# Third norm of a graph-network kernel: three blocks in flight, two chunks summed within it, and three DMA queues in a new order

## The chip, the cores and the metric

The kernel runs on one core of one Trainium2 chip. The metric is the device time of one execution in microseconds; each version is run several times and the median is compared.

## What the reference computes

The input is a matrix x of 3125 nodes by 128 features and a list of 100,000 edges (src, dst). Four graph networks follow one another, each behind a row-wise layer norm and a ReLU, and each adds to x:

```
h = max(layernorm(x), 0);  x = x + L0(h)     # sum over edges, two-layer network, log-softmax
h = max(layernorm(x), 0);  x = x + L1(h)     # two normalised graph convolutions
h = max(layernorm(x), 0);  x = x + L2(h)     # 4 layers: (A h + h) W1, ReLU, W2, batch norm, ReLU
h = max(layernorm(x), 0);  x = x + L3(h)     # h W0, S h W1, S S h W2; batch norm; the same again; a projection
```

A is the adjacency matrix of the edges. S is the transposed one with self loops, scaled on both sides by the inverse root of the degrees. What the change touches lies between the last layer of L2 and the first sum of L3: the last batch norm and ReLU of L2, the addition to x, the layer norm with its ReLU (this is the third norm after the first one), and the first product with S.

## The kernel before, in words

The adjacency matrix lies in SBUF as 25 tiles (`ADJ`, 125 rows by 3125 columns in bf16). A sum over edges is a dense product on TensorE: for a chunk of up to 4 tiles of target nodes (500 columns) it runs through the 25 tiles `t` of source nodes, with two matmuls for each: one with the high part and one with the low part of the node features, both 16 bit, which lie in `HP`. There are `NC` = 7 chunks, so a full sum has 350 matmuls (`sum_tiles`, line 1159). In L2 the chunks have 4, 4, 4, 4, 4, 3 and 2 tiles (`SPANS`), in the first sum of L3 the order is reversed: 2, 3, 4, 4, 4, 4 and 4 tiles (`SPANS3`), that is 250, 375 and five times 500 columns.

L3 needs the transposed adjacency `ADJT`. It is written over `ADJ` by seven DMA transposes from a copy in DRAM (`turned(c)`, line 1668), one for each chunk of columns. A transpose of chunk c may start when the last layer of L2 has summed its chunk c, since it overwrites those columns. The copy in DRAM is made earlier (`keep`, counted by `s_kept`).

L2's batch norm works feature by feature on the transposed data in `Zf`. After its factors are known (`s_bn["ab"]`), the work goes on in `NB` = 5 blocks of `BT` = 5 tiles: `relu(b)` on ScalarE (line 1878), `turn_block` on TensorE (five fp32 transposes into PSUM, line 1958, into one of the two slots of `RB3`), and on VectorE the addition to x (line 1986). Then comes the third norm of that block in `third_norm` on VectorE and `third_high` on ScalarE: statistics (lines 1100 and 1993), a square root on ScalarE (line 2014), a reciprocal and three small products on VectorE (lines 1999 to 2005). ScalarE then writes the high part of the five tiles to `HP` (line 2018) and, in fp32, four of the five tiles again to a scratch tile `GZ` (line 2024). VectorE makes the fifth (line 1973) and subtracts: low part = fp32 value minus high part (line 1979). There is one scratch tile, so ScalarE writes it only when the low part of the block before is done.

The L3 sum of TensorE waits block by block for `E3["hp"]`. Between the matmuls of chunk c, at set tiles `t`, TensorE does the dense products of chunk c-1, the hooks: `hidden1` (t = 4, line 2189), `back1` (t = 6, line 2195), `turned_h` (t = 12, line 2204) and `hidden0` (t = 17, line 2210). Each hook waits for results that VectorE and ScalarE make of the one before. `hidden1` waits for `E3["red"]` of its chunk, an operation of VectorE (line 2133) that multiplies the sum by a row of degree factors.

Queues are written out by hand. That of SyncE, in the stretch of interest, holds in this order: the last `row_piece` (line 1662), the transposes 0 to 3, `rows_out(s1_d)` (line 1658, a column of factors written to DRAM as 3125 numbers of 4 bytes), the transposes 4 and 5, the weights of L3 (line 2090, `s_wt`), transpose 6, and the six degree rows (`row_in`, line 2076), each a row of up to 500 numbers read for all 128 partitions. VectorE's first line 2133 waits for all six. The queue of ScalarE brings the first row of `s1_d` when the whole third norm is done.

Of the kernel before, what the change touches and what calls it, by code (L numbers as in the profile page):

```python
# [53 lines left out]
def build(nc, a, out):  # L54
# [75 lines left out]
    with ctx:  # L130
# [202 lines left out]
        s_dt, s_home, s_row = sem("s_dt"), sem("s_home"), sem("s_row")  # L333
# [727 lines left out]
        def layers(role, e, general, line):  # L1061
            pe, act, dve, pool, sp = (role == r for r in ("pe", "act", "dve", "pool", "sp"))
            done = lambda s, n: e.wait_ge(s, n + 1)
            if pool:
# [63 lines left out]
            def first_of(v, c, spans=SPANS):  # L1128
                return v[:, 0:spans[c][1] * PN]

# [17 lines left out]
            def sum_tiles(E_, H, c, accs, turned, group, before, spans=SPANS):  # L1148

                j0, nt = spans[c]  # L1150
                for t in range(NT):
                    before(t)
                    if turned:
                        cols = ADJT[0:PN, t, j0 * PN:(j0 + nt) * PN]
                    else:
                        cols = ADJ[0:PN, t, j0 * PN:(j0 + nt) * PN]
                    for q in range(2):
                        two = accs[0] is not accs[1]
                        mm = e.matmul(accs[q], H[0:PN, t, q, 0:P], cols, start=(t == 0 and (two or q == 0)),  # L1159
                                      stop=(t == NT - 1 and (two or q == 1)), skip_group_check=general)  # L1160
                if general:
                    for j in range(j0, j0 + nt):
                        with e.Fori(0, NT) as t:
                            remainder_landed(group, j * NT + t + 1)
                            for q in range(2):
                                mm = e.matmul(accs[q][:, (j - j0) * PN:(j - j0 + 1) * PN],
                                              H[0:PN, bass.ds(t, 1), q, 0:P].rearrange("p o f -> p (o f)"),
                                              LOT[0:PN, 0:PN], start=False, stop=True, skip_group_check=True)
                            mm.then_inc(s_lom, 1)
                    e.wait_ge(s_lom, (group * NT + j0 + nt) * NT + 1)  # L1170
                    e.sem_inc(E_["agg"], 1)
                else:
                    mm.then_inc(E_["agg"], 1)

# [476 lines left out]
            if sp:  # L1651
# [163 lines left out]
            def layer2(l, last):  # L1815
# [42 lines left out]
                if act:  # L1858
# [92 lines left out]
            def turn_block(l, b, ring=RB):  # L1951

                e.wait_ge(s_bn["rel"], l * NB + b + 1)
                if b >= 2:
                    done(E2["hp"], l * NB + b - 1)
                for m in range(BT):
                    c = (b * BT + m) * PN
                    mm = e.transpose(ring[b % 2][0:PN, m * P:(m + 1) * P], Zf[:, c:c + PN], IDF[:, :])  # L1958
# [5 lines left out]
            RB3 = [PS[:, 0:2, :].rearrange("p b c -> p (b c)"), PS[:, 2:4, :].rearrange("p b c -> p (b c)")]  # L1964
            MINE3 = BT - 1

            def third_norm():

                def low(b):
                    zb = GZ[0:PN].rearrange("p (t f) -> p t f", f=P)  # L1970
                    for m in range(MINE3, BT):
# [3 lines left out]
                    line.sync()  # L1975
                    done(E3["hi"], (b + 1) * BT)
                    e.wait_ge(s_z3, (b + 1) * MINE3)
                    ts = slice(b * BT, (b + 1) * BT)
                    e.scalar_tensor_tensor(out=HP[0:PN, ts, 1, 0:P], in0=zb, scalar=0.0, in1=HP[0:PN, ts, 0, 0:P],
                                           op0=ALU.max, op1=ALU.subtract).then_inc(E3["hp"], 1)  # L1980

                for b in range(NB):
                    ts = slice(b * BT, (b + 1) * BT)
                    e.wait_ge(s_bn["tr"], (LAYERS - 1) * NB + b + 1)
                    xb = XR[0:PN, ts, :]
                    line(e.tensor_tensor(xb, xb, RB3[b % 2][0:PN, 0:BT * P].rearrange("p (t f) -> p t f", f=P), ALU.add))
# [9 lines left out]
                    if b:  # L1996
                        low(b - 1)
# [10 lines left out]
                low(NB - 1)  # L2008

            def third_high(b):  # L2010

                ts = slice(b * BT, (b + 1) * BT)
                e.wait_ge(s_stat3, b + 1)
                e.activation(SDV[0:PN, ts], MV[0:PN, ts, 1], ACT.Sqrt, bias=EPSC[0:PN]).then_inc(s_sd3, 1)
                e.wait_ge(s_rs3, b + 1)
# [4 lines left out]
                if b:  # L2020
                    done(E3["hp"], b)
                for m in range(MINE3):
                    j = b * BT + m
# [9 lines left out]
            if pe:  # L2033
                for b in range(NB):
                    turn_block(LAYERS - 1, b, RB3)
            bank4 = PS[:, 4, :].bitcast(BF16)
# [37 lines left out]
            def row_in(tile, v, c, spans, to=s_dib):  # L2074
                j0, nt = spans[c]
                e.dma_start(first_of(tile, c, spans), bcast(v[j0 * PN:(j0 + nt) * PN])).then_inc(to, 16)

            def beside(c):

                return Zf[:, SPANS3[c + 1][0] * P:] if c + 1 < NC else GAT  # L2080

            def y1_of(c):
                return beside(c) if c + 1 < NC else LOS

            if sp:
                e.wait_ge(s_dout, 118)
                done(E2["agg"], NC * LAYERS)
                turned(NC - 2)
                done(E2["d2"], NC * LAYERS)
                e.dma_start(WB[:, 0:2 * P].rearrange("p (q n) -> p q n", q=2),  # L2090
                            a["L3_gnn_l1_w"][0:2].rearrange("q p n -> p q n")).then_inc(s_wt, 16)

                turned(NC - 1)
                e.wait_ge(s_bn["tr"], LAYERS * NB)
                for c in range(NC - 1):
                    row_in(beside(c), di_d, c, SPANS3)
# [26 lines left out]
            if dve:  # L2123
                for k in range(NC):
# [3 lines left out]
                    if k == 0:  # L2128
                        e.wait_ge(s_dib, dib0 + 16 * (NC - 1))
# [54 lines left out]
            if pe:  # L2184
# [29 lines left out]
                e.wait_ge(s_wt, wt0 + 16)  # L2214
                for c in range(NC):
                    def before(t):
                        if c == 0 and t % BT == 0:
                            done(E3["hp"], t // BT + 1)
                        if c == 1 and t == 0:
                            done(E2["hp"], LAYERS * NB)  # L2220
# [77 lines left out]
            if dve:  # L2298
                def joined(c):
# [3 lines left out]
                    e.wait_ge(s_dib, dib0 + 16 * (NC - 1) + 16 * n)  # L2303
# [296 lines left out]
```

## Time and profile before

| what | value |
|---|---|
| median of 3 runs | 1275.43 us (1274.34 to 1275.48) |
| the profiled execution, its own time | 1283.77 us |
| its span | 1282.1 us |
| TensorE busy | 1138.4 us, 89% of the span |
| VectorE, ScalarE, GpSimd busy | 686.7, 455.7, 8.5 us |
| mean granted clock of TensorE | 0.966 of full speed |

The profiled execution is 0.65% longer than the median. PE is TensorE's matmuls and PEld its weight loads, DVE is VectorE, ACT is ScalarE, POOL is GpSimd and SP is SyncE; an engine's name with a q is its queue, where DMAs are issued. A granted clock of 0.50 is 1.2 GHz and 1.00 is 2.4 GHz.

### The profile page before, as it was taken

The numbers are of one execution on the slowest core, as the hardware profiler recorded it, in microseconds if no ns is written. First come the engines' busy times: TensorE is split into PE (matmuls) and PEld (weight loads), VectorE is DVE, ScalarE is ACT, GpSimd is POOL, SyncE is SP. The second block draws the span as 40 slices with busy tenths as digits, with TensorE's granted clock in tenths as the row PEclk, the third lists the DMA queues.
The fourth block names the chain that finished last, engine by engine and source line by source line (L and its number), as shares of the span: only waits on it lengthen the run. The fifth ranks groups of instructions, "written<-read, shape, count | busy, mean of one in ns | idle before, by whom it ended". The sixth has DMA issues, their size and how long they took to land.

```text
span 1282.1 us, 19431 instructions
## 1 busy us (share of the span) xinstructions
PE 1138.4 (89%) x6308; PEld 660.5 (52%) x6308; DVE 686.7 (54%) x2175; ACT 455.7 (36%) x1348; POOL 8.5 (1%) x31
## 2 busy tenths in 40 slices
PE   1677899998979999998998998992699997899997
PEld 1556677664644555545445445451455554444644
DVE  8999999995452235545363453556144334532211
ACT  1558988895561112212113113116121113631100
POOL 1000000000000000000000000000000000000000
PEclk9999999999999999998998998995799998999999
DMA  3100000001001023333232231699622213410001
GB/s 62 32 2 2 2 2 10 2 1 46 6 11 24 21 54 74 88 70 74 42 68 55 51 85 30 139 198 213 153 60 63 85 38 80 111 47 23 13 24 29
DMA packets 208801, 70.31 MB, mean 55 GB/s; under 512 B 180999, under 2 KB 208074, under 8 KB 208699
## 3 DMA queue, kind: packets, MB, share of 16 engines
q1 hardware_dynamic: 121131, 43.37, 14.8%
q10 hardware_dynamic: 87568, 25.67, 9.4%
q8 instruction: 52, 0.85, 0.3%
q14 instruction: 50, 0.41, 0.1%
HBM read 20.71 MB, written 28.26 MB: 38 GB/s over the span
## 4 chain that ended last, share of the span: by engine, by line
PE 75%; DVE 10%; DMA 4%; SPq 4%; ACT 3%; issue 3%; DVEq 1%; ACTq 0%; POOL 0%; POOLq 0%
PE PS L1159 50%; PE PS L889 7%; DVE HPb L753 3%; SPq L1668 3%; PE PS L2425 2%; PE PS L1456 2%; PE PS L878 2%; PE PS L854 2%; PE PS L1922 2%; PE PS L1928 2%; DMA deg_d<-ADJ 1%; DVE HPb L704 1%; ACT HPb L2402 1%; DMA di_d<-SM 1%; ACT ADJ L925 1%
## 5 line engine op out<-in xcount | busy, mean ns | idle before, releaser
L1159 PE MATMUL PS<-ADJ,HPb 125*128 125x500 bf16 (+2 forms) x2450 | 490.5, 356 | 8.8 <-DMA WB<-in_L_gnn_l_w 4.3
L1159 PEld LDWEIGHTS PS<-ADJ,HPb 125*128 125x128 f16 x2450 | 240.4, 98 | 254.3 <-issue 40.5
L925 ACT CAST ADJ<-PS 126x72 f32 (+7 forms) x784 | 193.1, 315 | 51.6 <-PE PS L889 18.4
L1159 PE MATMUL PS<-ADJ,Zf 125*128 125x500 bf16 (+2 forms) x1050 | 202.1, 352 | 0.0
L889 PE MATMUL PS<-HPb 128*128 128x150 bf16 (+3 forms) x784 | 191.0, 345 | 3.6 <-ACT ADJ L925 2.5
L1159 PEld LDWEIGHTS PS<-ADJ,Zf 125*128 125x128 f16 x1050 | 102.4, 97 | 93.8 <-issue 1.3
L753 DVE TENSOR_SCALAR HPb<-XRf,Zf 128x176 bf16<-128x176 f16 (+2 forms) x588 | 135.2, 289 | 1.0 <-PE PS L889 0.2
L878 PEld LDWEIGHTS PS<-HPb 128*128 128x128 bf16 x642 | 86.0, 141 | 59.7 <-issue 34.3
L1727 DVE CUSTOM_DVE_ANT_0 HPb<-ADJ,HPb 125x625 bf16<-125x625 bf16 x125 | 101.2, 810 | 3.7
L878 PE MATMUL PS<-HPb 128*128 128x25 bf16 x642 | 90.9, 214 | 13.2 <-DVE HPb L753 12.5
L1826 DVE TENSOR_SCALAR Zf<-PS,B_L 128x500 f32<-128x500 f32 (+2 forms) x28 | 19.1, 682 | 141.5 <-PE PS L1928 141.5
L889 PEld LDWEIGHTS PS<-HPb 128*128 128x128 bf16 x784 | 86.0, 160 | 6.2 <-ACT ADJ L925 5.7
L1863 ACT ACTIVATE STW<-PS,SM 128x500 f32<-128x500 f32 (+2 forms) x28 | 17.7, 632 | 194.5 <-PE PS L1159 194.5
L704 DVE TENSOR_TENSOR HPb<-XRf,Zf 128x1750 bf16<-128x1750 f16 x56 | 59.6, 1064 | 0.6 <-DVEq L801 0.3
L753 DVE TENSOR_SCALAR HPb<-HPb,Zf 128x526 bf16<-128x526 f16 x196 | 54.4, 353 | 0.0
L2425 PE MATMUL PS<-HPb 128*125 128x384 f32 x114 | 42.4, 518 | 11.3 <-ACT HPb L2402 11.3
L1958 PE MATMUL PS<-IDF,Zf 128*125 128x128 f32 x100 | 20.7, 364 | 30.6 <-ACT Zf L1878 30.6
L883 PE MATMUL PS<-HPb 128*128 128x25 bf16 x142 | 26.6, 230 | 14.2 <-DVE HPb L753 13.2
L2171 ACT ACTIVATE HPb<-XRf,SM 125x128 f32<-125x128 f32 x25 | 10.4, 484 | 77.3 <-PE PS L2195 77.3
L2425 PEld LDWEIGHTS PS<-HPb 128*125 128x125 f32 x114 | 20.8, 195 | 32.3 <-ACT HPb L2402 20.8
L1868 ACT ACTIVATE SFG<-PS,B_L 128x500 f32<-128x500 f32 (+2 forms) x28 | 17.7, 632 | 54.2 <-PE PS L1922 54.2
L1958 PEld LDWEIGHTS PS<-IDF,Zf 128*125 128x125 f32 x100 | 18.5, 264 | 34.3 <-ACT Zf L1878 33.1
(325 smaller groups left out, 1022.9 us busy)
## 6 DMA issues: line engine op xcount, KB each, us to landing
adj_d<-ADJ ACTq DMA_DIRECT2D x25, 700.0 KB
HPb<-y_d SPq DMA_DIRECT2D x19, 187.5 KB, 2.5
HPb<-di_d SPq DMA_DIRECT2D x10, 250.0 KB, 3.8
adj_d<-ADJ ACTq DMA_DIRECT2D x25, 81.2 KB
ADJ<-in_x SPq DMA_DIRECT2D x1, 1562.5 KB
q_d<-HPb SPq DMA_DIRECT2D x25, 62.5 KB
HPb<-di_d SPq DMA_DIRECT2D x5, 305.2 KB
HPb<-s_d ACTq DMA_DIRECT2D x5, 250.0 KB, 3.9
```

The costliest lines, as they stand in the source:

```text
L704: e.tensor_tensor(OHP[h][:, 0:PN, :], IOC[:, 0:PN, :], PTH[:, n0:n0 + HC].rearrange("p (o c) -> p o c", o=1) .broadcast_to([P, PN, HC]), A ...
L753: e.tensor_scalar(OHK[k][:, 0:KWS[q]], IOK[q], KT[:, n0 + m:n0 + m + 1], None, ALU.is_equal)\
L854: mm = e.matmul(ACC0[c], PIECES[t][0:PN, q, :], ADJ[0:PN, t, j0 * PN:(j0 + nt) * PN], start=(r == 0), stop=(r == 2 * NT - 1), skip_group_c ...
L878: mm = e.matmul(to[:, :, bass.ds(places[g], 1)].rearrange("p t o -> p (t o)"), lhs, OHK[m % RING][:, 0:NT], start=False, stop=True, skip_g ...
L883: e.matmul(CPS[h][:, g * NT:(g + 1) * NT], lhs, OHK[m % RING][:, 0:NT], start=(c == 0), stop=(c == GC - 1), skip_group_check=True)
L889: e.matmul(WPS[group % BANKS][:, 0:rests * NT], OHP[h][:, :, g * GC + c], OHK[m % RING][:, NTP:KWS[q]], start=(c == 0), stop=(c == GC - 1) ...
L925: e.copy(to, WPS[group % BANKS][0:PD, t0 * RESTS[q]:t1 * RESTS[q]] .rearrange("p (t d) -> p t d", t=t1 - t0)).then_inc(s_mv, 1)
L1159: mm = e.matmul(accs[q], H[0:PN, t, q, 0:P], cols, start=(t == 0 and (two or q == 0)), stop=(t == NT - 1 and (two or q == 1)), skip_group_ ...
L1668: e.dma_start(ADJT[:, :, s0:s1], adj_d[s0:s1].rearrange("s t d -> s (t d)"), transpose=True)\
L1727: line(e.tensor_tensor_reduce(out=JUNK[0:PN], in0=ADJ[0:PN, t, r * PIECE:(r + 1) * PIECE], in1=ROWP[0:PN], scale=1.0, scalar=0.0, op0=ALU. ...
L1958: mm = e.transpose(ring[b % 2][0:PN, m * P:(m + 1) * P], Zf[:, c:c + PN], IDF[:, :])
L2425: mm = e.matmul(PS[0:PN, 4 + k % 2, 0:3 * P], YT[k][:, q, 0:PN], VW[:, q * 3 * P:(q + 1) * 3 * P], start=(q == 0), stop=(q == 2))
```

## The change

Third norm:
- TensorE's transposes go through three PSUM slots in place of two. It issues blocks 0 to 2 at once, and 3 and 4 from within the L3 sum.
- ScalarE does all five `relu` first. For each block it then makes the five tiles once, in fp32, into one of two scratch tiles (`ZB3`), and copies the whole block to the 16-bit high part in one operation. It also makes the next block's square root.
- VectorE makes no tile of its own. The order of its work is statistics of block b, low part of block b-2 (now a subtraction of two tensors), factors of block b.

L3 sum: chunks 0 and 1 are summed together (`sum_pair`), tile by tile, while the norm delivers blocks. The hooks of chunk 0 move from chunk 1 to chunk 2, those of chunks 1 and 2 into chunks 3 and 4, those of chunk 3 into chunk 4; from chunk 5 on they are where they were.

Queues: transpose 0 goes ahead of the last `row_piece`, `rows_out(s1_d)` behind transpose 4; the weights of L3 move from SyncE's queue to ScalarE's, and TensorE waits for them ahead of chunk 2 in place of chunk 0; the six degree rows move to GpSimd's queue, where they wait for the fifth transposed block and not for the transposes of the matrix. The row of chunk 0 goes to a place of its own in `LOS`.

The diff, cut to its core:

```diff
+            def beside(c):
+                return LOS[:, 2 * P:] if c == 0 else later_part(c) if c + 1 < NC else GAT
+            def y1_of(c):
+                return later_part(c) if c + 1 < NC else LOS
+            def later_part(c):
+                return Zf[:, SPANS3[c + 1][0] * P:]
+            def degree_rows():
+                e.wait_ge(s_dout, 118)
+                e.wait_ge(s_bn["tr"], LAYERS * NB)
+                for c in range(NC - 1):
+                    row_in(beside(c), di_d, c, SPANS3, s_drow)
...
                 else:
                     home()
+                    degree_rows()
...
+            def sum_pair(E_, H, group, before):
+                for t in range(NT):
+                    before(t)
+                    for c in range(2):
+                        j0, nt = SPANS3[c]
+                        for q in range(2):
+                            mm = e.matmul(sums3(c), H[0:PN, t, q, 0:P], ADJT[0:PN, t, j0 * PN:(j0 + nt) * PN],
+                                          start=(t + q == 0), stop=(t + q == NT), skip_group_check=True)
+                        if t == NT - 1 and not general:
+                            mm.then_inc(E_["agg"], 1)
...
                 for r in range(1, NB):
+                    if r == NB - 1:
+                        e.wait_ge(s_kept, 16 * (2 * NT + 1))
+                        done(E2["agg"], (LAYERS - 1) * NC + 1)
+                        turned(0)
                     e.wait_ge(s_dout, 17 * (r + 1))
                     row_piece(di_d, r)
...
-                e.wait_ge(s_kept, 16 * (2 * NT + 1))
-                for c in range(NC - 2):
-                    if c == NC - 3:
-                        e.wait_ge(s_dout, 102)
-                        rows_out(s1_d, DEG)
+                for c in range(1, NC - 2):
                     done(E2["agg"], (LAYERS - 1) * NC + c + 1)
                     turned(c)
+                e.wait_ge(s_dout, 102)
+                rows_out(s1_d, DEG)
...
                         if b + 1 < NB:
                             relu(b + 1)
-                        if last:
-                            third_high(b)
-                        else:
+                        if not last:
                             e.wait_ge(s_bn["tr"], l * NB + b + 1)
                             high_part("L2", b, turned_block(b))
+                    if last:
+                        done(E2["d2"], NC * LAYERS)
+                        e.dma_start(WB[:, 0:2 * P].rearrange("p (q n) -> p q n", q=2),
+                                    a["L3_gnn_l1_w"][0:2].rearrange("q p n -> p q n")).then_inc(s_wt, 16)
+                        for b in range(NB):
+                            third_high(b)
...
-                if b >= 2:
-                    done(E2["hp"], l * NB + b - 1)
+                if b >= len(ring):
+                    done(E2["hp"], l * NB + b + 1 - len(ring))
...
-            RB3 = [PS[:, 0:2, :].rearrange("p b c -> p (b c)"), PS[:, 2:4, :].rearrange("p b c -> p (b c)")]
-            MINE3 = BT - 1
+            RB3 = [PS[:, 2 * k:2 * k + 2, :].rearrange("p b c -> p (b c)") for k in (0, 1, 3)]
+            ZB3 = [v.rearrange("p (t f) -> p t f", f=P) for v in (Zf[0:PN, 0:BT * P], GZ[0:PN])]
...
-                def low(b):
...
-                        line(e.tensor_scalar(zb[:, m, :], XR[0:PN, j, :], RS[0:PN, j:j + 1], NBI[0:PN, j:j + 1],
-                                             ALU.mult, ALU.add))
...
-                    e.scalar_tensor_tensor(out=HP[0:PN, ts, 1, 0:P], in0=zb, scalar=0.0, in1=HP[0:PN, ts, 0, 0:P],
-                                           op0=ALU.max, op1=ALU.subtract).then_inc(E3["hp"], 1)
+                def low3(b):
+                    ts = block3(b)
+                    done(E3["hi"], b + 1)
+                    e.tensor_tensor(HP[0:PN, ts, 1, 0:P], ZB3[b % 2], HP[0:PN, ts, 0, 0:P], ALU.subtract)\
+                     .then_inc(E3["hp"], 1)
+                for b in range(NB):
+                    statistics3(b)
+                    if b >= 2:
+                        low3(b - 2)
+                    factors3(b)
+                low3(NB - 2)
+                low3(NB - 1)
...
             def third_high(b):
+                if b == 0:
+                    third_root(0)
+                    e.wait_ge(s_bn["tr"], (LAYERS - 1) * NB + 2)
                 e.wait_ge(s_rs3, b + 1)
+                if b >= 2:
+                    done(E3["hp"], b - 1)
                 for m in range(BT):
                     j = b * BT + m
-                    e.activation(HP[0:PN, j, 0, 0:P], tile_of(XR, j), ACT.Relu, bias=NBI[0:PN, j:j + 1],
-                                 scale=RS[0:PN, j:j + 1]).then_inc(E3["hi"], 1)
-                if b:
-                    done(E3["hp"], b)
-                for m in range(MINE3):
-                    j = b * BT + m
-                    e.activation(GZ[0:PN, m * P:(m + 1) * P], tile_of(XR, j), ACT.Relu, bias=NBI[0:PN, j:j + 1],
+                    e.activation(ZB3[b % 2][:, m, :], tile_of(XR, j), ACT.Relu, bias=NBI[0:PN, j:j + 1],
                                  scale=RS[0:PN, j:j + 1]).then_inc(s_z3, 1)
+                e.wait_ge(s_z3, (b + 1) * BT)
+                e.activation(HP[0:PN, block3(b), 0, 0:P], ZB3[b % 2], ACT.Copy).then_inc(E3["hi"], 1)
+                if b + 1 < NB:
+                    third_root(b + 1)
...
             if pe:
-                for b in range(NB):
+                for b in range(3):
                     turn_block(LAYERS - 1, b, RB3)
...
             if sp:
-                e.wait_ge(s_dout, 118)
                 done(E2["agg"], NC * LAYERS)
                 turned(NC - 2)
-                done(E2["d2"], NC * LAYERS)
-                e.dma_start(WB[:, 0:2 * P].rearrange("p (q n) -> p q n", q=2),
-                            a["L3_gnn_l1_w"][0:2].rearrange("q p n -> p q n")).then_inc(s_wt, 16)
                 turned(NC - 1)
-                e.wait_ge(s_bn["tr"], LAYERS * NB)
-                for c in range(NC - 1):
-                    row_in(beside(c), di_d, c, SPANS3)
                 done(E3["agg"], NC)
...
                     if k == 0:
-                        e.wait_ge(s_dib, dib0 + 16 * (NC - 1))
+                        e.wait_ge(s_drow, 16 * (NC - 1))
...
                 hooks = {4: hidden1, 6: back1, 12: turned_h, 17: hidden0}
-                e.wait_ge(s_wt, wt0 + 16)
-                for c in range(NC):
+                at = {2: {t: (h, 0) for t, h in hooks.items()},
+                      3: {3: (hidden1, 1), 5: (back1, 1), 10: (turned_h, 1), 13: (hidden0, 1), 18: (hidden1, 2),
+                          20: (back1, 2)},
+                      4: {1: (turned_h, 2), 4: (hidden0, 2), 8: (hidden1, 3), 10: (back1, 3), 15: (turned_h, 3),
+                          20: (hidden0, 3)}}
+                at.update({c: {t: (h, c - 1) for t, h in hooks.items()} for c in range(5, NC)})
+                for c in range(2):
+                    e.wait_ge(s_turned[c], 16)
+                def first_two(t):
+                    if t % BT == 0:
+                        b = t // BT
+                        if b + 3 < NB and not general:
+                            turn_block(LAYERS - 1, b + 3, RB3)
+                        done(E3["hp"], b + 1)
+                sum_pair(E3, HP, 4 + LAYERS, first_two)
+                for c in range(2, NC):
                     def before(t):
-                        if c == 0 and t % BT == 0:
-                            done(E3["hp"], t // BT + 1)
-                        if c and t in hooks:
-                            hooks[t](c - 1)
+                        if t in at[c]:
+                            hook, k = at[c][t]
+                            hook(k)
                     e.wait_ge(s_turned[c % 2], (c // 2 + 1) * 16)
+                    if c == 2:
+                        done(E2["hp"], LAYERS * NB)
+                        e.wait_ge(s_wt, wt0 + 16)
```

## Rows read from the trace of the kernel before

**Rows 1.** The page's chain that ended last, shares of the span.
```profile
PE 75%; DVE 10%; DMA 4%; SPq 4%; ACT 3%; issue 3%; DVEq 1%; ACTq 0%; POOL 0%; POOLq 0%
```

**Rows 2.** The chain in order of time, 860 to 1030 us: start, duration, what.
```profile
864.83 15.82 SPq L1668
...
880.75 13.30 SPq L1668
...
894.11 0.58 SPq L2090
...
894.74 13.31 SPq L1668
...
910.62 5.74 DMA Zf<-di_d
...
925.17 4.24 PE PS L1159 x24
...
937.17 5.08 PE PS L1159 x24
```

**Rows 3.** Instructions in order of time, SP queue: start, duration, what.
```profile
812.46 0.28 SPq L1662 DMA_DIRECT2D HPb<-di_d  x1
812.84 8.94 SPq L1668 DMA_TRANSPOSE ADJ<-adj_d  x1
...
861.33 19.32 SPq L1668 DMA_TRANSPOSE ADJ<-adj_d  x1
...
908.10 2.95 SPq L2076 DMA_DIRECT2D Zf<-di_d  x6
```

**Rows 4.** Instructions in order of time, the compute engines, 799 to 902 us.
```profile
799.62 0.68 ACT L1863 ACTIVATE STW<-PS,SM 128x500 f32<-128x500 f32 x1 [3.52 <-PE PS L1159]
...
871.10 2.50 PE L1958 MATMUL PS<-IDF,Zf 128*125 128x128 f32 x10 [3.68 <-ACT Zf L1878]
872.57 0.82 DVE L1986 TENSOR_TENSOR XRf<-XRf,PS 125x640 f32<-125x640 f32 x1 [2.52 <-PE PS L1958]
...
875.17 0.30 ACT L2014 ACTIVATE SM<-SM 125x5 f32<-125x5 f32 x1 [3.33 <-DVEq L1995]
875.50 0.19 DVE L1999 RECIPROCAL SM<-SM 125x5 f32<-125x5 f32 x1 [0.42 <-ACT SM L2014]
...
876.25 2.03 ACT L2018 ACTIVATE HPb<-XRf,SM 125x128 f16<-125x128 f32 x5 [0.79 <-DVEq L2007]
...
881.60 2.03 ACT L2018 ACTIVATE HPb<-XRf,SM 125x128 f16<-125x128 f32 x5 [0.79 <-DVEq L2007]
...
901.19 0.82 DVE L1979 SCALAR_TENSOR_TENSOR HPb<-HPb 125x640 f16<-125x640 f32 x1 [3.30 <-ACT HPb L2024]
```

**Rows 5.** Groups by line, 869.95 to 903 us: busy, mean ns | idle before.
```profile
L1878 ACT ACTIVATE Zf<-Zf,SM 128x625 f32<-128x625 f32 x5 | 4.4, 896 | 0.9 <-DVEq L1852 0.9
L1979 DVE SCALAR_TENSOR_TENSOR HPb<-HPb 125x640 f16<-125x640 f32 x5 | 4.1, 825 | 4.4 <-ACT HPb L2024 4.3
```

**Rows 6.** Groups by line, 937.1 to 1005 us, full-size chunks of the L3 sum.
```profile
L2155 DVE TENSOR_SCALAR SFG<-PS,B_L 128x500 f32<-128x500 f32 (+1 forms) x5 | 3.6, 713 | 13.8 <-PE PS L2210 13.8
L2121 DVE BATCH_NORM_STATS2 WB<-SFG 128x6 f32<-128x500 f32 (+1 forms) x5 | 3.3, 655 | 0.2
L2175 ACT ACTIVATE Zf<-STW 125x512 f16<-125x512 f32 x5 | 3.1, 630 | 1.2 <-DVE STW L2149 1.2
L2133 DVE SCALAR_TENSOR_TENSOR HPb<-PS,Zf 128x500 f32<-128x500 f32 x4 | 2.7, 679 | 8.0 <-PE PS L1159 8.0
```

**Rows 7.** PE by stretch: length, busy (instructions), granted clock, DMA share, GB/s.
```profile
897.00:901.00 4.00, 3.88 (x19) 0.50 1.25 284
901.00:902.00 1.00, 1.00 (x10) 0.87 1.33 303
905.00:908.00 3.00, 0.91 (x6) 1.00 1.26 281
```

**Rows 8.** DMA issues, 862 to 925 us: count, KB each, us to landing.
```profile
HPb<-s_d ACTq DMA_DIRECT2D x1, 125.0 KB, 6.7
```

More of the change, by code:

```diff
@@ L332, in build @@
         s_dout, s_dib, s_inv = sem("s_dout"), sem("s_dib"), sem("s_inv")
-        s_dt, s_home, s_row = sem("s_dt"), sem("s_home"), sem("s_row")
+        s_dt, s_home, s_row, s_drow = (sem("s_" + n) for n in ("dt", "home", "row", "drow"))
         s_first = sem("s_first")
@@ L1063, in layers, with first_of, row_in @@
             done = lambda s, n: e.wait_ge(s, n + 1)
+            def first_of(v, c, spans=SPANS):
+                return v[:, 0:spans[c][1] * PN]
+            def row_in(tile, v, c, spans, to=s_dib):
+                j0, nt = spans[c]
+                e.dma_start(first_of(tile, c, spans), bcast(v[j0 * PN:(j0 + nt) * PN])).then_inc(to, 16)
+            def beside(c):
[9 more added lines that the diff above has]
+                    row_in(beside(c), di_d, c, SPANS3, s_drow)
             if pool:
@@ L1173, in sum_tiles @@
                     mm.then_inc(E_["agg"], 1)
+            def sum_pair(E_, H, group, before):
[8 more added lines that the diff above has]
+                            mm.then_inc(E_["agg"], 1)
+                for c in range(2 if general else 0):
+                    j0, nt = SPANS3[c]
+                    for j in range(j0, j0 + nt):
+                        with e.Fori(0, NT) as t:
+                            remainder_landed(group, j * NT + t + 1)
+                            for q in range(2):
+                                mm = e.matmul(sums3(c)[:, (j - j0) * PN:(j - j0 + 1) * PN],
+                                              H[0:PN, bass.ds(t, 1), q, 0:P].rearrange("p o f -> p (o f)"),
+                                              LOT[0:PN, 0:PN], start=False, stop=True, skip_group_check=True)
+                            mm.then_inc(s_lom, 1)
+                    e.wait_ge(s_lom, (group * NT + j0 + nt) * NT + 1)
+                    e.sem_inc(E_["agg"], 1)
             def turn_back(E_, c, off=0):
@@ L1963, in layers, with block3, statistics3 @@
             RSU, NBU = MX, SE
-            RB3 = [PS[:, 0:2, :].rearrange("p b c -> p (b c)"), PS[:, 2:4, :].rearrange("p b c -> p (b c)")]
-            MINE3 = BT - 1
+            RB3 = [PS[:, 2 * k:2 * k + 2, :].rearrange("p b c -> p (b c)") for k in (0, 1, 3)]
+            ZB3 = [v.rearrange("p (t f) -> p t f", f=P) for v in (Zf[0:PN, 0:BT * P], GZ[0:PN])]
+            def block3(b):
+                return slice(b * BT, (b + 1) * BT)
             def third_norm():
-                def low(b):
-                    zb = GZ[0:PN].rearrange("p (t f) -> p t f", f=P)
-                    for m in range(MINE3, BT):
-                        j = b * BT + m
-                        line(e.tensor_scalar(zb[:, m, :], XR[0:PN, j, :], RS[0:PN, j:j + 1], NBI[0:PN, j:j + 1],
-                                             ALU.mult, ALU.add))
[L1975 to L1978, printed above, removed]
-                    e.scalar_tensor_tensor(out=HP[0:PN, ts, 1, 0:P], in0=zb, scalar=0.0, in1=HP[0:PN, ts, 0, 0:P],
-                                           op0=ALU.max, op1=ALU.subtract).then_inc(E3["hp"], 1)
-                for b in range(NB):
-                    ts = slice(b * BT, (b + 1) * BT)
+                def statistics3(b):
+                    ts = block3(b)
                     e.wait_ge(s_bn["tr"], (LAYERS - 1) * NB + b + 1)
                     xb = XR[0:PN, ts, :]
-                    line(e.tensor_tensor(xb, xb, RB3[b % 2][0:PN, 0:BT * P].rearrange("p (t f) -> p t f", f=P), ALU.add))
+                    line(e.tensor_tensor(xb, xb, RB3[b % 3][0:PN, 0:BT * P].rearrange("p (t f) -> p t f", f=P), ALU.add))
                     line.sync()
@@ L1995, in third_norm, with factors3 @@
                     e.sem_inc(s_stat3, 1)
-                    if b:
-                        low(b - 1)
+                def factors3(b):
+                    ts = block3(b)
                     e.wait_ge(s_sd3, b + 1)
@@ L2033, in layers @@
             if pe:
-                for b in range(NB):
+                for b in range(3):
                     turn_block(LAYERS - 1, b, RB3)
+                if general:
+                    for b in range(3, NB):
+                        turn_block(LAYERS - 1, b, RB3)
             bank4 = PS[:, 4, :].bitcast(BF16)
@@ L2072, in store @@
                 e.dma_start(y_d[q][:, j0 * PN:(j0 + nt) * PN], first_of(tile, c, spans)).then_inc(sem, 16)
[L2074 to L2083, printed above, removed]
             if sp:
-                e.wait_ge(s_dout, 118)
                 done(E2["agg"], NC * LAYERS)
                 turned(NC - 2)
-                done(E2["d2"], NC * LAYERS)
-                e.dma_start(WB[:, 0:2 * P].rearrange("p (q n) -> p q n", q=2),
-                            a["L3_gnn_l1_w"][0:2].rearrange("q p n -> p q n")).then_inc(s_wt, 16)
                 turned(NC - 1)
-                e.wait_ge(s_bn["tr"], LAYERS * NB)
-                for c in range(NC - 1):
-                    row_in(beside(c), di_d, c, SPANS3)
+                if general:
+                    degree_rows()
                 done(E3["agg"], NC)
```

17 lines of the change are left out of this document (6 added, 11 removed).

## The prediction

> **What bounds the kernel now.** I read the page's chain first: three quarters of the span are TensorE [rows 1], so the time is TensorE's work plus the places where it stands. Then the chain in order of time, where the norm lies. TensorE ends L2's last sum at 864.83, and from there the chain is SyncE's queue, not the norm: rest of transpose 4, transpose 5, the weights (894.11), transpose 6, and the degree rows, which land at 910.62 + 5.74 = 916.36 [rows 2]. TensorE stands twice behind this queue. Chunk 0 can't start before the weights: its matmuls begin at 897.12 (3.88 us busy of the 4 behind 897) [rows 7]. They reach the first `hidden1` at 905.91 (0.91 us busy behind 905) [rows 7], and that waits for line 2133, which waits for all six rows: 11 us. Under it lies a second limit. The norm delivers a block each 881.60 - 876.25 = 5.35 us and ends its last low part at 901.19 + 0.82 = 902.01 [rows 4]. A shorter queue alone would leave this one.
>
> The anchor is the start of chunk 2. The 24 matmuls from 925.17 are 16 of chunk 1 and 8 of chunk 2 [rows 2]. One of 500 columns takes 5.08 / 24 = 0.212 us [rows 2], 8 take 1.69, so chunk 2 starts at 925.17 + 4.24 - 1.69 = 927.72, the hooks of chunk 0 done. The 16 of 375 columns took 2.55, 0.159 each; half a full chunk, 250 columns, is 0.106. From here the chain is TensorE alone to beyond 1000 us, so what this point moves, the end moves.
>
> **SyncE's queue.** Transpose 0 may start when L2's last layer has summed chunk 0, at 799.6 (ScalarE takes that sum up then) [rows 4]; it takes 8.94 and ends at 808.6, before the `row_piece` at 812.46, which waits for VectorE [rows 3]. Cost nothing. Transposes 1 to 4 then run from 812.8, transpose 4 ends near 862, and `rows_out` follows. Transpose 4, right behind `rows_out`, took 19.32 [rows 3], the others 13.30: the small writes cost 6.0 us. They now fall on transpose 5. It waits for the end of the sum, 864.83, and ends at 884.2 (was 894.05); transpose 6 ends at 897.5 (was 908.05). Chunk 5, the first to need one of these, starts near 940. This cover is worth over 40 us.
>
> **The weights.** ScalarE issues them after five `relu` (4.4 us busy from 870.1 [rows 5], so 874.5), before the root that waits for statistics until 875.17 anyway [rows 4]. Even with the 6.7 us of a transfer beside a transpose [rows 8] they are there by 882; they are needed at 900. Cost nothing; TensorE's wait up to 897.12 goes.
>
> **The norm.** Per block VectorE has the statistics, 872.57 to 875.17 with the hand-over, 2.6; the factors, 875.50 to 876.25, 0.75 [rows 4]; the low part. That is another operation than before on the same shape; I take 0.83 [rows 5], and nothing in the rows makes it dearer. Sum 4.2. ScalarE has root 0.30 and five activations 2.03 [rows 4], and a copy of 640 columns that no row shows: 512 took 0.63 [rows 6], by length 0.74; bounds 0.63 and 0.94. With three hand-overs 3.3. So VectorE sets 4.2 in place of 5.35. In order:
> - Statistics 0 end at 875.1, factors 0 at 876.2, statistics 1 at 878.8. ScalarE: activations 0 to 878.3, copy to 879.1, root 1 to 879.4.
> - Factors 1 to 880.2, statistics 2 to 882.8, low part 0 to 883.7.
> - Factors 2 to 884.4, statistics 3 to 887.0, low part 1 to 887.9, factors 3 to 888.7.
> - Statistics 4 need the last transposes (below): 889.1 to 891.7; low part 2 to 892.5; factors 4 to 893.3; low part 3 to 894.1.
> - ScalarE's activations 4 end at 895.3, the copy at 896.1, low part 4 at 897.0, five us before the 902.01 of now.
>
> **The paired sum.** A block is 10 matmuls of 250 and 10 of 375 columns: 2.65 us at 1.00, 5.3 at 0.50. The number of matmuls is the same; that a tile now alternates between two PSUM banks has no row, and I take nothing, since the loads are as many. The clock is at 0.50 when the first block comes, at 883.7. After the start at 897.12 it stayed there 4.0 us and read 0.87 in the next [rows 7]. So 4 us at half, the rest at full: 888.4. Then the five transposes of block 4, 0.7 to 1.25 (ten took 2.50 at half clock [rows 4]): 889.1. Block 1 ends at 891.8, block 2 waits for 892.5 and ends at 895.2, block 3 at 897.8, block 4 at 900.5.
>
> **Chunk 2 and the moved hooks.** Chunk 2 starts at 900.5, but now holds chunk 0's hooks. Before, 34 matmuls (7.2) and the four hooks of chunk 1 lay between 927.72 and 937.17 [rows 2]: hooks 2.25 for 375 columns, 1.5 for 250. So TensorE gains 927.7 - 900.5 - 1.5 = 25.7. One moved pair is tight: in chunk 4, `hidden0` of chunk 2 (t = 4) and `hidden1` of chunk 3 (t = 8) have 8 matmuls between them, 1.7 us, in which VectorE does lines 2155, 2121 and 2133, 0.71 + 0.66 + 0.68 = 2.05 [rows 6] and hand-overs. I take a wait of 0.5. Left: 25.2.
>
> **The degree rows on GpSimd's queue.** They may start when block 4 is transposed, 889.1; line 2133 needs all six at 901.7, so that `hidden1` runs at its place, 900.5 + 8 x 0.212 = 902.2. GpSimd issues no DMA in this trace, so its price has no row. Lower bound: SyncE's six issues, 2.95 [rows 3], a landing of 5.74 behind the last [rows 2]: 897.3. Upper bound: each waits for the one before to land, 6 x 5.74, until 923.5. The rows also share the engines with transpose 6: the six move 1.31 MB, at 281 GB/s [rows 7] 4.7 us; behind all of transpose 6 they would end at 902.2. The nearest row is the same DMA from another queue, so I take up to 1 us each: last issue 894.1, landed 899.9, cost nothing.
>
> A rule of the Trainium skill speaks against this part: SBUF — State Buffer, section Who interferes with whom, says that a DMA issued from GpSimd can be held up by VectorE's copies and tensor_scalar operations, since both use a shared port. The page gives 3.1 us in place of 0.62 for such a transfer. By it the sum would lose what the rival below loses. No row here bears on it; VectorE's work in this stretch is mostly of other kinds, which the page lets pass.
>
> **ScalarE's row of `s1_d`** leaves after low part 4, 897.4, and with 6.7 us [rows 8] lands at 904.1. Line 2138 then runs 1.5 late, and the next to wait is `turned_h` at t = 12, which TensorE reaches at 906.4; VectorE needs some 2 us, until 906.1. Cost nothing; anything later costs one for one.
>
> **Sum.** -25.2. The profiled execution goes from 1283.77 to 1258.6. The median of the runs is 0.65% lower, which changes the difference by 0.2: 1275.4 to 1250.3.
>
> **Rivals.**
> - *GpSimd's issues are dear.* At 3.1 us each, midway between the bounds, the last leaves at 904.6 and lands at 910.3; `hidden1` waits 8.6, the clock falls in such a gap and half clock for 4 us costs 2 more: 1261. For it: no row; against: VectorE isn't copying. Chance 0.08.
> - *The other side: dearer still.* The whole gain is gone when the last row lands at 925, which is 6 us an issue. At 7 it lands at 929.8: 28.1 + 2 lost, 1280. Against it: SyncE's 0.49 each [rows 3], even a full landing each is below. Chance 0.03; near 6 us, no change: 0.02.
> - *The clock stays at half through the paired sum*, since the blocks come in bursts. Five blocks at 5.3 and 1.25 of transposes end at 911.5: 11 later, 1261. Against: at half clock a block lasts longer than VectorE's 4.2, so TensorE has no gap. Chance 0.05.
> - *The norm keeps its period* by hand-overs I miss: low part 4 at 883.7 + 4 x 5.35 = 905.1, chunk 2 at 907.8: 1257.5. Chance 0.07.
>
> My forecast has the rest, 0.75. Its own range, from the copy's bounds, a wait of 0 to 1 in each hook moved, and rows up to 4 us late, is 1248 to 1254. The 8 in 10 range reaches to the slower rivals: 1247 to 1261. About 0.2% can be told from no change; faster 0.95, same 0.02, slower 0.03.
>
> **What would show it.** In the new trace: the low parts about 4.2 us apart with the last ending near 897; the paired matmuls from 884 to 900 without a gap over 1 us and a clock of 1.00 from 888; the first 500-column matmul near 900.5; no idle time ahead of the first `hidden1`; transpose 6 over near 897.5. Wrong it would be by a wait of line 2133 for the degree rows, by new waits ahead of hooks in chunks 3 and 4, or by a paired sum at half clock.

## The result, and the profile after

The changed kernel takes 1255.46 us (median of 4 runs, 1255.11 to 1258.08) against 1275.45 us: a ratio of 0.9845, interval 0.9825 to 0.9865, 20.0 us. In a later comparison on a chip where both runs were longer and spread wider it was 1257.33 us against 1280.30, ratio 0.9813 (0.9795 to 0.9832), 23.0 us. The forecast was 1250.3 us, 25.2 less, with a range of 1247 to 1261.

In the page's chain that ended last, by engine, SyncE's queue (SPq) has gone from 4% to 0% (compare [rows 1]):

```profile
PE 78%; DVE 12%; ACT 5%; issue 3%; DMA 1%; DVEq 1%; ACTq 0%; POOL 0%; POOLq 0%; SPq 0%
```

Two traces of the same kernel differ by up to 8.4 us ahead of the changed part, as shown further below, so I compare a stretch in each trace: from ScalarE's last pass over L2's last sum (line 1863 before; this instant is called the mark) to the last `hidden1` of the L3 sum. Before it is 996.37 - 864.85 = 131.5 us, after 968.51 - 860.18 = 108.3: 23.2 less. Second traces of both kernels show 131.5 and 108.4. What follows the stretch takes 285.7 and 285.0 us.

The new trace in order of time, the stretch of the norm and of the paired sum (start, duration, engine, line; in brackets the idle time before and what ended it). To put a time beside [rows 4], add 4.67, the distance of the two marks:

```profile
878.50 0.83 DVE L2054 TENSOR_TENSOR HPb<-Zf,HPb 125x640 f16<-125x640 f32 x1 [0.50 <-ACT HPb L2083]
...
879.38 4.45 PE L1203 MATMUL PS<-ADJ,HPb 125*128 125x250 bf16 x20 [8.32 <-DVE HPb L2054]
...
882.69 0.83 DVE L2054 TENSOR_TENSOR HPb<-HPb 125x640 f16<-125x640 f32 x1
...
883.67 0.71 PE L2009 MATMUL PS<-IDF,Zf 128*125 128x128 f32 x5
...
884.21 2.83 PE L1203 MATMUL PS<-ADJ,HPb 125*128 125x250 bf16 x20
...
885.66 2.64 POOL L1069 DMA_DIRECT2D Zf<-di_d  x5
...
887.07 0.83 DVE L2054 TENSOR_TENSOR HPb<-Zf,HPb 125x640 f16<-125x640 f32 x1
...
887.96 8.18 PE L1203 MATMUL PS<-ADJ,HPb 125*128 125x250 bf16 x60 [0.91 <-DVE HPb L2054]
...
891.39 0.83 DVE L2054 TENSOR_TENSOR HPb<-Zf,HPb 125x640 f16<-125x640 f32 x1 [1.95 <-ACT HPb L2083]
...
895.97 1.85 PE L1180 MATMUL PS<-ADJ,HPb 125*128 125x500 bf16 x8
896.87 0.42 DVE L2179 SCALAR_TENSOR_TENSOR HPb<-PS,HPb 128x250 f32<-128x250 f32 x1 [4.65 <-DMA Zf<-di_d]
...
900.94 0.47 DVE L2184 SCALAR_TENSOR_TENSOR Zf<-HPb,B_L,PS 128x250 f32<-128x250 f32 x1 [3.65 <-DMA HPb<-s_d]
...
903.36 0.41 PE L2250 MATMUL PS<-IDF,HPb 125*128 125x125 f32 x2 [1.28 <-ACT HPb L2217]
```

The low parts (line 2054) start 4.2 and 4.4 us apart, then 1.6 and 2.8 (the fourth, at 888.62, is left out here), in place of 5.35 throughout. The last ends at 892.2, 32.0 us after the mark (before: 37.2 [rows 4]). TensorE sums nearly without a gap from 879.4 to 896.1, and chunk 2 starts at 895.97. The stretches below give length, then busy time and instructions of PE, PEld, DVE, ACT and POOL, then granted clock, DMA share and GB/s. The first has a mean clock of 0.66, the next ones 1.00, the full 2.4 GHz. Taken us by us, the clock is 0.50 until 882, 0.65 in the next us and 1.00 from 883, so TensorE worked at half clock for about 3.3 us of its first paired block:

```profile
880.00:884.00 4.00, 4.00 (x22) 2.60 (x21) 3.57 (x16) 2.94 (x7) 0.00 (x0) 0.66 1.30 227
884.00:888.00 4.00, 3.09 (x25) 2.10 (x24) 3.34 (x14) 3.07 (x7) 3.01 (x6) 1.00 1.29 201
888.00:896.00 8.00, 8.00 (x61) 5.82 (x62) 2.06 (x5) 2.77 (x6) 0.30 (x1) 1.00 1.13 268
```

From the start of chunk 2 TensorE waits in two places only (engine, line, waited for: us, times, longest), `turned_h` of chunk 0 and `hidden1` of chunk 3:

```profile
PE PS L2250 <- ACT HPb L2217: 1.3, 1, 1.3
PE PS L2235 <- DVE HPb L2179: 0.4, 1, 0.4
```

Two transfers landed late (count, KB each, us to landing); compare [rows 8]. The degree rows hold up VectorE's line 2179 (4.65 us idle in the listing above), but TensorE's 8 matmuls of chunk 2 cover that. The row of `s1_d` holds up line 2184, and this is what `turned_h` waits behind:

```profile
Zf<-di_d POOLq DMA_DIRECT2D x4, 250.0 KB, 8.6
...
HPb<-s_d ACTq DMA_DIRECT2D x1, 125.0 KB, 8.6
```

Both were in flight together with transpose 6, which held SyncE's queue for 19.39 us, until 897.05:

```profile
877.66 19.39 SPq L1713 DMA_TRANSPOSE ADJ<-adj_d  x1
```

### The profile page after: what moved, and what is told of

It is laid out like the page before. It is cut to its first block, busy times and chain, and to the rows that moved or that the text cites. A ratio compares the mean times of both kernels' runs of the same rounds, so it can differ in the third digit from the quotient of the medians.

```text
span 1253.5 us, 19410 instructions
## 1 busy us (share of the span) xinstructions
PE 1134.7 (91%) x6308; PEld 658.5 (53%) x6308; DVE 684.4 (55%) x2170; ACT 452.2 (36%) x1333; POOL 11.8 (1%) x37
## 4 chain that ended last, share of the span: by engine, by line
PE 78%; DVE 12%; ACT 5%; issue 3%; DMA 1%; DVEq 1%; ACTq 0%; POOL 0%; POOLq 0%; SPq 0%
PE PS L1180 50%; PE PS L889 7%; DVE HPb L753 4%; PE PS L1501 3%; PE PS L2487 2%; PE PS L878 2%; PE PS L854 2%; PE PS L1973 2%; PE PS L1979 2%; DVE HPb L704 1%; ACT HPb L2464 1%; PE PS L1438 1%; PE PS L2009 1%; ACT ADJ L925 1%; PE PS L1430 1%
## 5 line engine op out<-in xcount | busy, mean ns | idle before, releaser
L1180 PE MATMUL PS<-ADJ,HPb 125*128 125x500 bf16 (+2 forms) x2350 | 472.2, 356 | 4.5 <-DVE HPb L1367 2.7
L1180 PEld LDWEIGHTS PS<-ADJ,HPb 125*128 125x128 f16 x2350 | 228.7, 98 | 242.5 <-issue 36.9
L878 PEld LDWEIGHTS PS<-HPb 128*128 128x128 bf16 x642 | 86.1, 141 | 59.6 <-issue 34.1
L889 PEld LDWEIGHTS PS<-HPb 128*128 128x128 bf16 x784 | 85.8, 159 | 6.2 <-ACT ADJ L925 5.5
L883 PE MATMUL PS<-HPb 128*128 128x25 bf16 x142 | 26.5, 230 | 14.2 <-DVE HPb L753 13.2
L2487 PEld LDWEIGHTS PS<-HPb 128*125 128x125 f32 x114 | 20.7, 194 | 31.8 <-ACT HPb L2464 20.5
L883 PEld LDWEIGHTS PS<-HPb 128*128 128x128 bf16 x142 | 19.4, 140 | 21.5 <-issue 13.4
```

Source lines behind the costliest of these rows:

```text
L878: mm = e.matmul(to[:, :, bass.ds(places[g], 1)].rearrange("p t o -> p (t o)"), lhs, OHK[m % RING][:, 0:NT], start=False, stop=True, skip_g ...
L883: e.matmul(CPS[h][:, g * NT:(g + 1) * NT], lhs, OHK[m % RING][:, 0:NT], start=(c == 0), stop=(c == GC - 1), skip_group_check=True)
L889: e.matmul(WPS[group % BANKS][:, 0:rests * NT], OHP[h][:, :, g * GC + c], OHK[m % RING][:, NTP:KWS[q]], start=(c == 0), stop=(c == GC - 1) ...
L2487: mm = e.matmul(PS[0:PN, 4 + k % 2, 0:3 * P], YT[k][:, q, 0:PN], VW[:, q * 3 * P:(q + 1) * 3 * P], start=(q == 0), stop=(q == 2))
```

## The experiments

In the table, in us: from the mark to the first `hidden1` of the L3 sum and to the last one, both from one profiled execution each, and the median with its ratio to the kernel before on the same chip. The runs were made on several chips, so the ratios are compared and not the medians. The first two lines have two traces each.

| kernel | first | last | gain in the stretch | median | ratio (interval) |
|---|---|---|---|---|---|
| before | 52.1, 52.3 | 131.5, 131.5 | | 1280.3 | 0.9994 (0.9975 to 1.0014) |
| changed | 37.5, 37.5 | 108.3, 108.4 | 23.2 | 1257.33 | 0.9813 (0.9795 to 0.9832) |
| queues only | 39.6 | 116.6 | 14.9 | 1268.21 | 0.9875 (0.9845 to 0.9905) |
| norm and pair only | 54.3 | 126.6 | 5.0 | 1274.29 | 0.9926 (0.9897 to 0.9955) |
| unpaired | 35.6 | 118.3 | 13.2 | 1270.42 | 0.9913 (0.9883 to 0.9944) |
| old norm in new order | 41.6 | 111.0 | 20.5 | 1264.34 | 0.9875 (0.9850 to 0.9901) |
| transpose 6 late | 37.4 | 106.8 | 24.7 | 1254.97 | 0.9802 (0.9783 to 0.9821) |
| row of `s1_d` early | 37.5 | 106.8 | 24.7 | 1257.08 | 0.9819 (0.9798 to 0.9840) |
| both, hooks of chunk 3 later | 37.6 | 106.5 | 25.0 | 1255.89 | 0.9804 (0.9786 to 0.9823) |
| that, unpaired | 34.7 | 111.7 | 19.8 | 1262.58 | 0.9849 (0.9816 to 0.9882) |

**The kernel before, once more.**

> The kernel before, unchanged. Its profiled execution took 1283.77 us, 8.3 more than the median of the runs, while the changed kernel's profiled execution is as fast as its other runs. Between the two traces the stretch from ScalarE's last pass over L2's last sum to the last hidden1 of the L3 sum is 131.7 us before and 108.5 after, 23.2 less, but the medians differ by 20.0. Theory: the first trace before was long by some 3 us in this stretch too, since its chain there is made of DMA transposes whose length varies, so this trace shows about 128.5 us. Rival: the stretch is 131.7 again and the medians hide a loss of 3 us elsewhere in the changed kernel. Time: 1274 to 1277 us.

The theory fell: the stretch is 131.5 us again. No trace shows the rival's loss either: behind the stretch the changed kernel takes as long on average (285.0 and 286.5 us in its two traces, 285.7 and 285.6 before), and in the second comparison the medians differ by 23.0. What varies lies ahead of the mark, where but for the place of transpose 0 both kernels do the same. Between 300 and 600 us, in a hook of the second network, TensorE waits for a product of VectorE: in the kernel before, in the changed kernel, and in the changed kernel's second trace (one line of the waits of each):

```profile
PE PS L1527 <- DVE HPb L1495: 3.5, 2, 3.3
```

```profile
PE PS L1572 <- DVE HPb L1540: 0.2, 1, 0.2
```

```profile
PE PS L1572 <- DVE HPb L1540: 4.4, 2, 4.2
```

It is there in one trace of the changed kernel and not in the other, and the mark lies at 864.9, 860.2 and 868.6 us in these three. Behind TensorE's wait stands a transfer: VectorE's product (line 1540, before 1495) waits for a row of `di_d`, 3.7 us in the first of these traces, not at all in the second, 6.4 us in the second trace of the kernel before (not among the three), and in the third:

```profile
DVE HPb L1540 <- DMA HPb<-di_d: 4.7, 1, 4.7
```

Why this row lands at different times was not settled. Nor can the 20.0 us of the first comparison be split, since the profiled execution of before was 8 us above the median of its other runs.

**The changed kernel, once more**, as the mark for the three runs beside it.

> The changed kernel, unchanged, as the mark for the three beside it: 1255.5 us, 20 us faster than before.

23.0 us faster here, 23.2 in the stretch.

**Queues only.** The diff's hunks for SyncE, GpSimd and line 2133's wait on the kernel before; in addition

```diff
+                        if last and b == 0:
+                            done(E2["d2"], NC * LAYERS)
+                            e.dma_start(WB[:, 0:2 * P] ...).then_inc(s_wt, 16)
                         if last:
                             third_high(b)
```

> Only the queues of the change (transpose 0 early, the small writes behind transpose 4, weights on ScalarE's queue, degree rows on GpSimd's); norm and sums as before. Theory: the old norm is the next limit. Its last low part ends as before, 37.2 us after the end of L2's sum (902.0 on the old clock), chunk 0 of the sum ends 1 us later, chunk 1 with its hooks takes 9.5 us, so chunk 2 starts near 912.6 in place of 927.7: 15 us faster, 1260.5 us. Rival: the two waits of TensorE for SyncE's queue were the whole of it and the norm hides, 22 us or more faster; or the norm's new form matters most, under 8 us faster.

14.9 us in the stretch, where the theory had 15. In its trace TensorE waits for the last low part, which ends at 903.54, 37.2 us after the mark (866.37), as before:

```profile
902.72 0.82 DVE L2005 SCALAR_TENSOR_TENSOR HPb<-HPb 125x640 f16<-125x640 f32 x1 [3.30 <-ACT HPb L2050]
```

```profile
903.60 2.51 PE L1179 MATMUL PS<-ADJ,HPb 125*128 125x250 bf16 x18 [2.59 <-DVE HPb L2005]
```

The degree rows leave at 894.93 here, when transpose 6 is nearly through, and it holds SyncE's queue for 11.59 us in place of the 19.39 of the changed kernel:

```profile
884.60 11.59 SPq L1688 DMA_TRANSPOSE ADJ<-adj_d  x1
```

**Norm, pair and hooks only.** The changed kernel with SyncE's queue as before:

```diff
-                    degree_rows()                      # GpSimd's queue
...
                 turned(NC - 2)
+                done(E2["d2"], NC * LAYERS)
+                e.dma_start(WB[:, 0:2 * P] ...).then_inc(s_wt, 16)
                 turned(NC - 1)
+                degree_rows()
```

> Only the new norm, the paired sum and the moved hooks; SyncE's queue in its old order, with the weights and, last, the degree rows. Theory: TensorE sums chunks 0 and 1 by 900.5 on the old clock as in the full change, then hidden1 of chunk 0 waits for the degree rows until 916.9 in place of 902.2, and half clock after the gap costs 2 more: 25.2 - 14.7 - 2 = 8.5 us faster, 1267 us. Rival: everything stays behind the queue, no gain above 3 us; or the queue isn't what sets it, and the gain is above 15 us.

5.0 us in the stretch, where the theory had 8.5: its mechanism, with a smaller gain. Line 2175 is its `E3["red"]`:

```profile
PE PS L2231 <- DVE HPb L2175: 17.0, 2, 16.6
```

```profile
892.40 15.00 SPq L1712 DMA_TRANSPOSE ADJ<-adj_d  x1
```

Transpose 6 takes 15.0 us in place of 13.3, and `hidden1` comes 54.3 us after the mark, 2.2 later than in the kernel before, where the theory took the same time. Most of the remaining 1.3 us of the difference is the clock behind the gap of 16.6 us. It reads 0.50 until 921 and 1.00 from 922, so TensorE works at half clock for some 5.8 us, where the theory took 4. Four matmuls of 500 columns take 0.47 us each, twice their 0.21 and the last one's end:

```profile
916.83 1.87 PE L1179 MATMUL PS<-ADJ,HPb 125*128 125x500 bf16 x4
```

**Unpaired.** Hooks at `{c: {t: (h, c - 1)}}` for every chunk again, and

```diff
-                sum_pair(E3, HP, 4 + LAYERS, first_two)
-                for c in range(2, NC):
+                for c in range(NC):
                     def before(t):
+                        if c == 0:
+                            first_two(t)
```

> The changed kernel with the two first chunks summed one after the other again and every hook at its old place; new norm and new queues stay. Theory: chunk 0 is paced by the norm and ends 1 us after the last low part, near 898 on the old clock; all of chunk 1 (8.0 us) and its hooks (1.5) follow, so chunk 2 starts at 907.5 with them done, against 902.0 in the changed kernel: 5.5 us slower than the changed kernel, 1261 us. Less a wait of 1.3 us for turned_h of chunk 0 that the changed kernel has; if this wait stays, 5.5; if it goes, 4.2. Rival: TensorE would wait for the norm in either order, and the pairing is worth under 2 us.

10.0 us slower than the changed kernel in the stretch, not 5.5. TensorE reaches `turned_h` of chunk 0 while the row of `s1_d` is still on its way:

```profile
895.56 0.69 PE L2235 MATMUL PS<-HPb,WB 128*128 128x250 f32 x2 [0.72 <-DVE HPb L2179]
...
903.09 0.65 PE L2250 MATMUL PS<-IDF,HPb 125*128 125x125 f32 x2 [3.85 <-ACT HPb L2217]
```

**Transpose 6 late.** On SyncE's queue:

```diff
                 turned(NC - 2)
+                e.wait_ge(s_row, 16)
                 turned(NC - 1)
```

> The changed kernel, but transpose 6 waits on SyncE's queue until the first row of s1_d has landed. In the changed kernel this row takes 8.6 us to land and the degree rows 7.7 to 8.6, while transpose 6 is in flight; TensorE then waits 1.28 us for turned_h of chunk 0. Theory: the transfers share the DMA engines with the transpose. With it out of the way the row lands in under 4.5 us, the wait of 1.28 us goes, 1.3 us faster than the changed kernel; transpose 6 lands near 912 on the new clock, before chunk 6 needs it at 950. Rival: the landing is slow for another reason (the number of descriptors, the queue), it stays above 7 us and the time stays the same.

1.5 us less in the stretch. Without the transpose beside them the same transfers land in about half the time or less:

```profile
Zf<-di_d POOLq DMA_DIRECT2D x4, 250.0 KB, 4.5
...
HPb<-s_d ACTq DMA_DIRECT2D x1, 125.0 KB, 2.9
```

So the long landings of the changed kernel come from sharing with transpose 6, not from the queue or the shape.

**The row of `s1_d` early.** `beside(0)` becomes `HID`, and in `degree_rows`, with VectorE's counts moved by one:

```diff
                 e.wait_ge(s_dout, 118)
+                row_in(LOS[:, 2 * P:], s1_d, 0, SPANS3, s_drow)
                 e.wait_ge(s_bn["tr"], LAYERS * NB)
```

> The changed kernel, but the first row of s1_d goes to a place of its own and leaves on GpSimd's queue ahead of the degree rows, some 20 us before it is needed; the degree row of chunk 0 goes to HID. Transpose 6 stays where it is. Theory: the wait of 1.28 us goes since the row has landed long before, 1.3 us faster than the changed kernel. Rival: VectorE's chain from hidden1 to turned_h is as long as TensorE's 8 matmuls anyway, and under 0.5 us is won.

Again 1.5 us less in the stretch: the other way to take the same wait away. The row itself, now beside transpose 5 and ahead of all degree rows, still took 7.4 us to land; it was only early enough. The medians can tell neither this version nor the one with transpose 6 late from the changed kernel.

**Both, and later hooks.** The two edits together, transpose 6 waiting for `s_drow`, and `9: (hidden1, 3), 11: (back1, 3), 17: (turned_h, 3), 22: (hidden0, 3)` in chunk 4.

> Both of these, transpose 6 waiting for the degree rows, and the hooks of chunk 3 one or two tiles later in chunk 4 (9, 11, 17, 22). Theory: besides the 1.28 us the wait of 0.43 us ahead of hidden1 of chunk 3 goes: 1.7 us faster than the changed kernel, 1253.8 us. Rival: later hooks push a wait into chunk 5, and no more is won than by s1_early.

1.8 us less than the changed kernel in the stretch, and no wait of TensorE from chunk 2 to the last hook. It is the shortest stretch of all and beats both kernels there; by the medians (1255.89 and 1257.33) it can't be told from the changed kernel.

**The old norm in the new order.** The old `third_norm`, `third_high` and two-slot `RB3` in the changed kernel, with

```diff
-                        if b + 3 < NB and not general:
-                            turn_block(LAYERS - 1, b + 3, RB3)
+                        if b + 2 < NB and not general:
+                            turn_block(LAYERS - 1, b + 2, RB3)
```

> The changed kernel with the old norm inside it: two PSUM slots, one scratch tile, relu by relu, 5.35 us a block; the paired sum, the moved hooks and the new queues stay. Measured so far, from ScalarE's last pass over L2's sum to the last hidden1: 131.5 us before, 108.35 in the changed kernel, 116.6 with the queues alone. Theory: low part 4 comes 5.1 us later than in the changed kernel (37.2 against 32.0 after the mark), chunk 2 starts 4.1 us later (the paired sum has slack it didn't have), the rows have landed by then: 112.3. Rival: norm and pairing only work together, and the stretch is near the 116.6 of the queues alone; or the norm is worth nothing behind the paired sum, and it stays near 108.4.

111.0 us, 2.6 more than the changed kernel; the theory had 112.3. Blocks 3 and 4 of the paired sum wait for the norm, the one for 2.03 us with the clock falling (4.51 us for 20 matmuls), the other for 0.69:

```profile
894.03 4.51 PE L1203 MATMUL PS<-ADJ,HPb 125*128 125x250 bf16 x20 [2.03 <-DVE HPb L2030]
899.23 2.84 PE L1203 MATMUL PS<-ADJ,HPb 125*128 125x250 bf16 x20 [0.69 <-DVE HPb L2030]
```

Chunk 2 starts at 901.9, 39.9 after the mark (35.8 in the changed kernel): the 4.1 of the theory. The rows have landed by then, so the wait for `turned_h` goes, which gives back 1.3.

**Early rows, unpaired.**

> The version with the early row of s1_d and the late transpose 6 (106.5 us in the stretch), but chunks 0 and 1 summed one after the other and the hooks at their old places. Without the pairing, the changed kernel's stretch was 118.3 us, 10.0 longer and not 5.5. Theory: 4.5 of these 10 are waits for rows that the pairing happened to cover (hidden1 and turned_h of chunk 0 come earlier in the sum, 0.7 + 3.8 us of waits against 1.3, and the clock falls behind them). With the rows early and the transpose out of the way they go, and the pairing itself is worth 5.5: 112.0. Rival: the pairing itself is worth 10, and the stretch stays near 116.5.

The version above, both edits, without the pairing. 111.7 us, 5.1 more than its paired twin (106.5). The pairing itself is worth about that. Of the 10.0 us above, the other 4.9 came with the late rows: without the pairing TensorE waited 4.6 us for them, with a granted clock of 0.70 on average from 904 to 908 us behind it; with the pairing it waited 1.3 us. About 0.3 of the 5.1 is not the pairing but the later hooks of the twin (106.5 against 106.8).

## Why the prediction was right, point by point

- *SyncE's queue was what bound, with the norm close behind.* Shown: the queues alone give 14.9 us, and the trace stops at the old norm's end, 37.2 after the mark; norm and pair alone give 5.0 and stop at the degree rows. Neither alone comes near the 23.2.
- *The norm.* Right: last low part 32.15 us after the mark by the prediction, 32.0 in the trace. The copy that no row showed took 0.74, the subtraction 0.83, both as taken.
- *The paired sum.* Right: chunk 2 at 900.5 on the old clock; measured 895.97 + 4.67 = 900.64. The clock was at half for about 3.3 us of the first block (forecast 4) and full from there. The alternation between two banks costs little: 20 matmuls take 2.83 with the last one's end, the 60 together 8.18, 2.7 a block (2.65 forecast).
- *The degree rows on GpSimd's queue.* Right in the result, and in part by luck. GpSimd issues the six in 3.3 us, 0.68 for the first and 0.53 for each of the others, against 2.95 for the six on SyncE. Both rivals on a dear issue are out. The rule of the Trainium skill (SBUF — State Buffer, Who interferes with whom) on a DMA held up behind VectorE has hardly a case here: beside the issues VectorE ran mainly statistics, an addition and a subtraction of two tensors, which the page lets pass, and the trace agrees at 0.53 us an issue. With the queues only, one tensor_scalar of VectorE (0.35 us) falls among the five issues, and they take 2.65 us, no longer; no run put copies beside them. But the rows landed in 8.6 us and not in 5.74, late enough to delay line 2179 by 1.1 (36.7 after the mark, 35.6 with transpose 6 late), all of it inside the cover of 8 matmuls. Two errors offset each other: had an issue cost the 1 us that I took, the last row, leaving at 894.1 and landing 8.6 later, would have been there at 902.7, 1.0 too late.
- *The step that was mis-sized: the row of `s1_d`.* I took 6.7 us from a row of the kernel before and found its consequences just covered. It took 8.6, and `turned_h` waited 1.28 us. Two experiments that remove the cause in different ways both give 1.5 us back.
- *The sign that did not come: transpose 6.* I had it over near 897.5; it left SyncE's queue at 897.05 + 4.67 = 901.7. Transpose 5 was over earlier than I had it (882.3 against 884.2), but transpose 6 took 19.39 us in place of 13.3. I had counted what the transpose does to the degree rows and not what they do to it. Where the rows leave when it is nearly through, with the queues only, it takes 11.6 us. So the row of `s1_d`, issued at 892.25 + 4.67 = 896.9, met nearly five us of transpose 6, where by my own times the two hardly overlapped. Beside a transpose alone such a row took 6.7 us (before) and 7.4 (the row early), with no transpose in the queue 3.0 (queues only); that the degree rows make up the difference to 8.6 is not shown by a run of its own.
- *The tight pair of hooks.* Right: 0.43 us waited, 0.5 forecast; moved hooks remove it.
- *The rest.* 25.2 less 1.28 is 23.9, the stretch gained 23.2. The 0.7 left is small change that I read off the trace without testing it: chunk 2 starts 0.1 later, and at each of the two waits 0.2 to 0.3 are lost besides the idle time, in the end of the last matmul before it (12 take 2.71 us, 12 x 0.212 is 2.54) and in a longer first one behind it (`hidden1` of chunk 3: 1.11 in place of 1.00).
- *The median.* It moved by 20.0 in the first comparison and 23.0 in the second. The stretch says 23.2 in the first pair of traces and 23.1 in the second; the 3 us between the comparisons are left open.

## What to carry to other kernels

Where a chain runs through a queue, read what stands right behind it before valuing the fix: here queue and norm bound within 15 us of each other, and each alone gave 5 or 15 of 23. A transfer that is moved meets other neighbours, so its landing time from the old trace binds in neither direction (6.7 us became 8.6, and 2.9 or 3.0 without a transpose in the queue), and the neighbours get longer too. Here it paid, by 1.5 us in the stretch, to hold back a bulk transfer that nobody needed yet until the small urgent ones had landed. When whole runs spread more than the effect, measure from a mark to a mark inside the trace.

## What the runs showed that I had not expected

The same 125 KB row took 8.6 us beside a transpose and 2.9 without; four 250 KB rows 8.6 and 4.5. Transpose 6 took 19.4 us beside them and 11.6 nearly alone. Pairing two chunks was worth 5.1 us by itself and nearly as much again (10.0 in all) where rows were late.
